# The transform of the tail: per sequence, by products of 64 rows and 64 columns, on the upper and the lower half of TensorE

## The chip, the cores and the metric

The kernel runs on one core of one Trainium2 chip. A core has TensorE (PE; its weight loads are shown as PEld), VectorE (DVE), ScalarE (ACT), GpSimd (POOL) and a queue that issues DMAs (SP). The metric is the device time of one execution in microseconds: the kernel before takes 1292.83 us, the median of 3 runs that lie between 1289.83 and 1294.05.

## The reference

Two layers are computed over 128 sequences of 64 tokens with 128 channels, `x` and a context `ctx` of the same shape:

```
x = x + L0_xattn(layernorm(x), ctx, ctx)      # softmax attention, 16 heads of 8
x = x + L0_ffn(layernorm(x))                  # 64 experts, the 8 best of each token, and a shared one
x = x + L1_xattn(layernorm(x), ctx, ctx)      # the part that the change touches
x = x + L1_ffn(layernorm(x))                  # ternary weights, one product
```

The third line correlates queries and keys along the sequence by Fourier transforms, and mixes shifted copies of the values:

```
Q, K, V = _linear(query, Wq, bq), _linear(key, Wk, bk), _linear(value, Wv, bv)   # split into heads
corr = irfft(rfft(Q, axis=seq) * conj(rfft(K, axis=seq)), n=64, axis=seq)
top_w, top_idx = top_k(corr.mean(axis=-1), 4)                                    # int(log(65)) = 4 delays
out = sum_i softmax(top_w)[i] * roll(V, top_idx[i], axis=seq)
out = _linear(out, Wo, bo)
```

## The kernel before, in words

A tile is 128 rows by 128 channels: two sequences of 64 tokens, one in partitions 0 to 63, the other in 64 to 127. There are 64 tiles. Everything stays in SBUF from one layer to the next. `attention` works through the tiles first, `experts` through 33 pairs of experts in 16 chunks of tiles, then `tail` does the third layer and what precedes the fourth, and `ternary` the last product and the stores.

`tail` works on pairs of tiles, 32 pairs, in a software pipeline of 46 steps that is written out in program order for each engine. In step s the pair n = s - 1 is transformed, n = s - 2 is projected, n = s - 3 is multiplied on POOL, and so on up to the pair s - 13. What precedes what within a step is the order of the `if on(s, lag)` blocks in each engine's function; semaphores tie the engines together.

TensorE's order in a full step is: output projection of pair s - 11 (L1547, L1548), in every fourth step the transpose of the delays' weights (L1553), the transform of pair s - 1 (L1561), the inverse transform of pair s - 10 (L1573), two transposes (L1581), in every fourth step L1587, the projections of pair s - 2 (L1594 to L1596, once for each tile of the pair), and in every fourth step the correlation (L1606).

The transform is what changes. For each of the four sources of a pair (tile 0 and 1 of the normed x, tile 0 and 1 of the context) the source is the stationary operand, 128 rows of tokens by 128 channels, and a 128x128 table `cst["dft"][:, 0:P]` moves through. The table holds the two sequences' transforms in blocks, so its result has the channels as partitions and 128 columns in which frequency and sequence alternate: column 2f + b is frequency f of sequence b. Half of the table's numbers are zeros, since each sequence is transformed by itself. A product of two f32 operands is carried out as two instructions for TensorE, each with its own weight load, so the four products of a pair appear as eight loads and eight matmuls. The results of a pair fill one PSUM bank, and there are two such banks, `pf[0]` and `pf[1]`, used in turn: the transform of pair n waits until ScalarE has copied pair n - 2 out (`at_least(pe, f_out, n - 1)`). ScalarE's copy (L1501) takes the 512 columns to `l_xf` in SBUF, from which the projections read.

ScalarE's order in a step is: L1496 in every fourth step, the copy L1501, the exponential L1505 in every fourth step, L1510, L1514 in every fourth, L1520, L1526, and then the copies of the projections, L1535 to L1537 (for the first eight pairs once per tile, then once per pair).

The tables come in by DMAs that SP issues once, with the fourth tile of `attention` (L225).

Of the kernel before, what the change touches and what calls it, by code (L numbers as in the profile page):

```python
# [22 lines left out]
F32 = mybir.dt.float32  # L23
# [66 lines left out]
def attention(nc, cst, dram, x, ctxT, x_res, raw, held, norms, routing, sem, n_tiles=TILES):  # L90
# [7 lines left out]
    with ExitStack() as mem:  # L98
# [99 lines left out]
        late_weights = [(w1[:, k, :], dram[name]) for k, name in enumerate(("Wq1", "Wk1", "Wv1", "Wo1"))] + [  # L198
            (wt_raw, dram["wt"]), (bo1row[:], dram["bo1"].unsqueeze(0)), (bv1col[:], dram["bv1"].unsqueeze(1))]
        tables = [(cst["eb"][:], dram["eb"].unsqueeze(0).to_broadcast([P, E]))]  # L200
        tables += [(cst[name][:], dram[name]) for name in ("dft", "idft_corr", "idft_conv")]
        tables += [(cst[name][:], dram[name].unsqueeze(1)) for name in ("ln_gamma", "ln_beta")]
        tables += [(braw[:, k, :], dram[name].unsqueeze(0).to_broadcast([3, D])) for k, name in ((0, "bq1"), (1, "bk1"))]

# [973 lines left out]
def dft_tables():  # L1178

    f = np.concatenate([np.arange(S // 2 + 1), np.arange(1, S // 2)])
    second = np.arange(S) > S // 2
    angle = 2 * np.pi * np.outer(f, np.arange(S)) / S
    cos, sin = np.cos(angle), np.sin(angle)
    weight = np.where((f == 0) | (f == S // 2), 1.0, 2.0)[:, None] / S
    sign = np.where(second, -1.0, 1.0)[:, None]
    alone = ((f == 0) | (f == S // 2))[:, None]
    rows = lambda m: np.kron(np.eye(2), m).reshape(2, S, P).transpose(1, 0, 2).reshape(P, P)  # L1190
    cols = lambda m: rows(m).T
    return {

        "dft": np.concatenate([cols(np.where(second[:, None], -sin, cos)), cols(np.where(second[:, None], cos, -sin))], 1),

        "idft_corr": np.concatenate([rows(np.where(alone, 0.0, weight * sign * sin)), rows(weight * cos)], 1) / HD,

        "idft_conv": np.concatenate([rows(weight * sign * cos), rows(-weight * sin)], 1),
    }
# [25 lines left out]
def tail(nc, cst, entry, x_res, y_mean, y_rstd, xnT, amax, sem):  # L1225
# [15 lines left out]
    with ExitStack() as mem:  # L1241
# [3 lines left out]
        def psum(name, shape):  # L1245
            return mem.enter_context(nc.psum_tensor(name, shape, F32))
# [23 lines left out]
        y_mv = sb("l_y_mv", [P, 4, 2])  # L1270
        y_ve = sb("l_y_ve", [P, 4])

        pf = [psum(f"l_pf{i}", [P, 2, 2, P]) for i in range(2)]
        pq = psum("l_pq", [P, 2, 512])[:, :, 0:3 * D].rearrange("p j (c d) -> p j c d", d=D)
        po = psum("l_po", [P, 2, P])
        py = psum("l_py", [P, 2, D])
# [56 lines left out]
        with nc.Block() as block:  # L1333
# [155 lines left out]
            @block.scalar  # L1489
            def _(act):  # L1490
                for s in range(STEPS):
                    g = group(s, 9)
                    if g is not None:
                        act.wait_ge(w_turned, g + 1)
                        at_least(act, c_transformed, g)
                        nc.scalar.copy(cT[:], pw).then_inc(w_out, 1)  # L1496
                    if on(s, 1):
                        n = s - 1
                        act.wait_ge(transformed, n + 1)
                        at_least(act, projected, 2 * (n - 1))  # L1500
                        nc.scalar.copy(xf[:, n % 2], pf[n % 2][:]).then_inc(f_out, 1)  # L1501
                    k = group(s, 8)
                    if k is not None:
                        act.wait_ge(shifted, k + 1)
                        nc.scalar.activation(e[:], e[:], ACT.Exp).then_inc(exped, 1)  # L1505
                    if on(s, 10):
                        n = s - 10
                        act.wait_ge(inverted, n + 1)
                        at_least(act, o_projected, n - 1)
                        nc.scalar.copy(oT[:, n % 2], po[:]).then_inc(o_out, 1)  # L1510
                    if g is not None:
                        act.wait_ge(c_transformed, g + 1)
                        at_least(act, mixed, 4 * (g - 1))
                        nc.scalar.copy(cf[:, g % 2].rearrange("p i t h -> p i (t h)"), pab).then_inc(c_out, 1)  # L1514
                    if on(s, 12):
                        n = s - 12
                        act.wait_ge(rooted, 2 * n + 2)
                        at_least(act, z_turned, n - 1)
                        for j in range(2):
                            ins = nc.scalar.activation(zn[:, n % 2, j, :], x_res[:, 2 * n + j, :], ACT.Identity,  # L1520
                                                       bias=offset[:, n % 2, j:j + 1], scale=rstd[:, n % 2, j:j + 1])
                        ins.then_inc(z_normed, 1)
                    if on(s, 13) and s - 13 >= DRAINED:
                        n = s - 13
                        act.wait_ge(z_turned, n + 1)
                        nc.scalar.activation(xnT[:, 2 * n * P:2 * (n + 1) * P], pt[:], ACT.Identity,  # L1526
                                             bias=cst["ln_beta"][:], scale=cst["ln_gamma"][:]).then_inc(z_out, 1)
                    if on(s, 2):
                        n = s - 2
                        at_least(act, mixed, n - SLOTS + 1)  # L1530
                        at_least(act, products, n - SLOTS + 1)
                        for tiles in ((0, 1), (1, 2)) if n < APART else ((0, 2),):
                            some = slice(*tiles)
                            act.wait_ge(projected, 2 * n + tiles[1])
                            nc.scalar.copy(qkv[:, n % SLOTS, some, 1:4, :], pq[:, some])  # L1535
                            nc.scalar.copy(qkv[S:, n % SLOTS, some, 0, :], pq[0:S, some, 1, :])
                            nc.scalar.copy(qkv[0:S, n % SLOTS, some, 0, :], pq[S:, some, 1, :]).then_inc(q_out, tiles[1] - tiles[0])  # L1537

            @block.tensor
            def _(pe):  # L1540
                for s in range(STEPS):
# [12 lines left out]
                    if on(s, 1):  # L1554
                        n = s - 1
                        pe.wait_ge(normed, n + 1)
                        pe.wait_ge(loaded[n % 4], 16 * (n // 4 + 1))
                        at_least(pe, f_out, n - 1)
                        for j in range(2):
                            for i, src in enumerate((xn[:, n % 2, j], cin[:, n % 4, j])):  # L1560
                                ins = nc.tensor.matmul(pf[n % 2][:, j, i, :], src, cst["dft"][:, 0:P], start=True, stop=True)  # L1561
                        ins.then_inc(transformed, 1)
                    if s == 1:
                        for j in range(4):
# [146 lines left out]
def two_layers(nc, d, out):  # L1711

    with ExitStack() as mem:
        def sb(name, shape, dt=F32):
            return mem.enter_context(nc.sbuf_tensor(name, shape, dt))

        def sem(name):
            return mem.enter_context(nc.semaphore(name))

        shapes = {  # L1720
            "ident": ([P, P], F32), "hmask": ([P, 4], F32), "maskq": ([P, P], BF16),
            "maskk": ([P, 4 * S], BF16), "ones": ([P, P], F32), "mhalf": ([P, 1], F32),
            "Wq": ([D, D], F32), "Wo": ([D, D], F32), "bqc": ([P, 1], F32), "boe": ([P, D], F32),
            "centT": ([D, E], F32), "eb": ([P, E], F32),
            "w1T": ([D, 4, D], F32), "bias3": ([P, 4, D], BF16), "first_rows": ([P, P], BF16), "ones3": ([P, P], BF16),
            "dft": ([P, 2 * P], F32), "idft_corr": ([P, 2 * P], F32), "idft_conv": ([P, 2 * P], F32),
            "ln_gamma": ([D, 1], F32), "ln_beta": ([D, 1], F32), "beta": ([P, 1], F32), "wt": ([D, D], F32),
        }
        cst = {name: sb(name, shape, dt) for name, (shape, dt) in shapes.items()}
        x_res = sb("x_res", [P, TILES, D])  # L1730
        rows = "(t p) s d -> t (p s) d"
        x = d["x"].rearrange(rows, p=2)
        ctx = d["ctx"].rearrange(rows, p=2)
        y_mean = sb("y_mean", [P, TILES])
        y_rstd = sb("y_rstd", [P, TILES])
        held = sb("held", [P, 2048])
        entry = Entry(nc, held, ctx, sem)
        with ExitStack() as ffn:
            for name in ("wuh", "wul", "wdh", "wdl"):
                cst[name] = ffn.enter_context(nc.sbuf_tensor(name, [P, PAIRS * P], F32R))  # L1740
            raw = ffn.enter_context(nc.sbuf_tensor("raw", [P, 2, PAIRS * P], F32))
            norms = ChunkNorm(nc, ffn, sem)
            routing = Routing(nc, ffn, sem, cst, raw, norms)
            attention(nc, cst, d, x, d["ctxT"], x_res, raw, held, norms, routing, sem)
            experts(nc, cst, x_res, norms, routing, entry, y_mean, y_rstd, sem)
        xnT2 = sb("xnT2", [P, TILES * P])
        amax = sb("amax", [P, TILES // 2])
        tail(nc, cst, entry, x_res, y_mean, y_rstd, xnT2, amax, sem)
        ternary(nc, cst, x_res, xnT2, amax, out.rearrange(rows, p=2), sem)

# [32 lines left out]
```

## Time and profile before

| | us |
|---|---|
| median of 3 runs | 1292.83 |
| the profiled execution, its own time | 1293.18 |
| its span, first to last instruction | 1291.3 |
| first transform of the tail (L1561) | starts at 1106.7 |
| last one | starts at 1228.8 |

All times in the profile are of one execution. They count from the span's start. TensorE's granted clock, as a share of full speed, is 0.985 over the span and 1.00 from 1106 to 1230 us. A matmul's recorded duration has a fixed part in it, since matmuls overlap in the array: eight matmuls of 275 ns each take 1.06 us together, not 2.2. The pace at which they follow each other is read from the starts, or from the time of a group.

### The profile page before, as it was taken

What the parts mean: (1) busy time and instruction counts of PE and PEld (TensorE: products, weight loads), DVE (VectorE), ACT (ScalarE), POOL (GpSimd) and SP (SyncE); (2) the same over time, 40 slices, a digit from 0 to 9 for tenths busy, and PEclk for the clock granted to TensorE, in tenths of its full rate; (3) what the DMA queues carried; (4) which work ended last, traced back from release to release, by engine and by line L of the source; (5) the groups of instructions that cost most, each with busy time, mean ns of one, the idle gap of its engine ahead of it and who ended that gap; (6) DMA issues with size and microseconds to landing.
All of it is one profiled execution on the core that took longest, in us unless ns stands there. A gap on an engine that the chain in (4) does not pass through costs nothing. (4 is left out here: it accounts for less than half of the span.)

```text
span 1291.3 us, 29811 instructions
## 1 busy us (share of the span) xinstructions
PE 1240.9 (96%) x9114; PEld 998.2 (77%) x9114; DVE 1066.5 (83%) x2061; ACT 922.4 (71%) x1525; POOL 769.2 (60%) x828
## 2 busy tenths in 40 slices
PE   7999999996999999999999999999999999899986
PEld 4777777775788888788878878788878888799975
DVE  4878888886788879779879889779889787689986
ACT  3778888884777777676767777777777777777761
POOL 3775665662556556656657556656657533477773
PEclk9999999997999999999999999999999999999998
DMA  4511111100976776876866876876877777111004
GB/s 119 114 31 31 30 28 32 29 20 3 213 184 165 184 181 154 193 169 151 195 162 171 192 170 165 189 175 160 186 169 178 184 181 182 34 34 30 22 2 131
DMA packets 126149, 159.56 MB, mean 124 GB/s; under 512 B 20840, under 2 KB 59504, under 8 KB 126064
## 3 DMA queue, kind: packets, MB, share of 16 engines
q1 hardware_dynamic: 124974, 158.16, 50.3%
q8 instruction: 34, 0.56, 0.2%
q10 hardware_dynamic: 1090, 0.43, 0.1%
q14 instruction: 51, 0.42, 0.1%
HBM read 152.25 MB, written 6.29 MB: 123 GB/s over the span
## 5 line engine op out<-in xcount | busy, mean ns | idle before, releaser
L1036 DVE TENSOR_TENSOR e_m<-e_pu,raw 128x1024 f32<-128x1024 f32 x256 | 309.8, 1211 | 94.6 <-ACT e_pu L1099 67.7
L1099 ACT ACTIVATE e_pu<-e_pu 128x1024 f32<-128x1024 f32 x256 | 258.6, 1010 | 161.7 <-PE e_pu L1135 160.0
L1109 ACT CAST e_mh<-e_m 128x1024 fp32r<-128x1024 f32 x256 | 268.0, 1047 | 46.3 <-DVE e_m L1036 45.4
L955 POOL TENSOR_TENSOR e_ml<-e_m,e_mh 128x1024 fp32r<-128x1024 f32 x80 | 192.9, 2415 | 125.3 <-ACT e_mh L1109 125.1
L1041 DVE TENSOR_TENSOR e_ml<-e_m,e_mh 128x1024 fp32r<-128x1024 f32 x176 | 238.6, 1356 | 21.6 <-ACT e_mh L1109 20.8
L1133 PE MATMUL e_pu<-r_xh,wuh 128*128 128x512 f32 x528 | 215.1, 407 | 2.3 <-PEq L208 1.9
L1144 PE MATMUL e_py<-e_mh,wdh 128*128 128x512 f32 x528 | 208.4, 395 | 3.0 <-ACT held L1086 3.0
L1134 PE MATMUL e_pu<-r_xh,wul 128*128 128x512 f32 x528 | 209.4, 397 | 0.0
L1135 PE MATMUL e_pu<-r_xl,wuh 128*128 128x512 f32 x528 | 209.3, 396 | 0.0
L1145 PE MATMUL e_py<-e_mh,wdl 128*128 128x512 f32 x528 | 209.1, 396 | 0.0
L1148 PE MATMUL e_py<-e_ml,wdh 128*128 128x512 f32 x528 | 168.2, 397 | 1.0 <-DVE e_ml L1041 0.4
L1144 PEld LDWEIGHTS e_py<-e_mh,wdh 128*128 128x128 f32 x528 | 99.1, 188 | 27.7 <-issue 4.2
L1148 PEld LDWEIGHTS e_py<-e_ml,wdh 128*128 128x128 f32 x528 | 98.1, 188 | 28.6 <-POOL e_ml L955 4.1
L1133 PEld LDWEIGHTS e_pu<-r_xh,wuh 128*128 128x128 f32 x528 | 99.8, 189 | 25.1 <-issue 2.3
L1135 PEld LDWEIGHTS e_pu<-r_xl,wuh 128*128 128x128 f32 x528 | 99.8, 189 | 24.2
L1145 PEld LDWEIGHTS e_py<-e_mh,wdl 128*128 128x128 f32 x528 | 99.1, 188 | 24.4
L1134 PEld LDWEIGHTS e_pu<-r_xh,wul 128*128 128x128 f32 x528 | 100.0, 189 | 21.1
L377 POOL TENSOR_TENSOR kx<-qkT,hmask 128x512 f32<-128x512 f32 x64 | 66.5, 1039 | 80.2 <-ACT qkT L479 78.3
L267 DVE TENSOR_REDUCE mx<-ps 128x16 f32<-128x1024 f32 x64 | 78.3, 1224 | 43.3 <-PE ps L530 43.3
L569 PEld LDWEIGHTS pob<-vx,pT 128*64 128x64 f32 x2048 | 66.2, 139 | 27.7 <-issue 21.2
L272 DVE TENSOR_TENSOR prob<-ps,mx 128x1024 f32<-128x1024 f32 x64 | 77.6, 1212 | 0.1
L569 PE MATMUL pob<-vx,pT 128*64 128x18 f32 x2048 | 72.4, 214 | 2.3 <-DVE x_res L289 1.5
(232 smaller groups left out, 2358.5 us busy)
## 6 DMA issues: line engine op xcount, KB each, us to landing
raw<-gates_scratch SPq DMA_DIRECT2D x512, 256.0 KB, 4.3
x_res<-in_x_dram SPq DMA_DIRECT2D x64, 64.0 KB, 1.8
xcT<-in_ctxT_dram SPq DMA_DIRECT2D x64, 64.0 KB, 1.9
held<-in_ctx_dram SPq DMA_DIRECT2D x32, 128.0 KB, 2.1
out_dram<-t_res SPq DMA_DIRECT2D x16, 256.0 KB, 2.8
raw<-in_L_ffn_W_up_dram SPq DMA_DIRECT2D x4, 512.0 KB, 4.3
raw<-in_L_ffn_W_down_dram SPq DMA_DIRECT2D x4, 512.0 KB, 5.8
gates_scratch<-raw SPq DMA_DIRECT2D x16, 128.0 KB, 2.3
```

Source lines behind the costliest of these rows:

```text
L569: ins = nc.tensor.matmul(po[q, 2 * j:2 * j + 2, :], pT[:, r % 2, j, q], vx[:, r % 4, j, b], start=True, stop=True)
L955: nc.gpsimd.tensor_tensor(flat(ml[k][:]), flat(m[k][:]), flat(mh[k][:]).bitcast(F32), ALU.subtract).then_inc(m_low[1], 1)
L1036: nc.vector.tensor_tensor(flat(m[r % 3][:]), flat(pu[r % 3][:]), flat(gt[i % SPREAD]), ALU.mult).then_inc(gated, 1)
L1041: nc.vector.tensor_tensor(flat(ml[k][:]), flat(m[k][:]), flat(mh[k][:]).bitcast(F32), ALU.subtract).then_inc(m_low[0], 1)
L1099: nc.scalar.activation(flat(pu[k][:]), flat(pu[k][:]), ACT.Silu).then_inc(silued, 1)
L1109: nc.scalar.copy(flat(mh[k][:]), flat(m[k][:])).then_inc(m_high, 1)
L1133: nc.tensor.matmul(pu[k][:, j, :], cst["wuh"][:, w], xh[:, b, :], start=True, stop=False)
L1134: nc.tensor.matmul(pu[k][:, j, :], cst["wul"][:, w], xh[:, b, :], start=False, stop=False)
L1135: ins = nc.tensor.matmul(pu[k][:, j, :], cst["wuh"][:, w], xl[:, b, :], start=False, stop=True)
L1144: nc.tensor.matmul(py[:], cst["wdh"][:, w], mh[k][:, j, :], start=(i == 0 and j == 0), stop=False)
L1145: nc.tensor.matmul(py[:], cst["wdl"][:, w], mh[k][:, j, :], start=False, stop=False)
L1148: ins = nc.tensor.matmul(py[:], cst["wdh"][:, w], ml[k][:, j, :], start=False, stop=(i == FULL))
```

## The change

The two sequences of a tile are transformed by products of their own. Each takes 64 rows of the source (partitions 0 to 63, or 64 to 127) as the stationary operand, 64 rows by 128 channels, and moves a 64x64 table through, which stands twice in `dft_half`, once in each half of the partitions. The product for sequence 0 lies on the upper half of TensorE's rows and writes to the first bank of `pf`, the one for sequence 1 on the lower half and to the second bank. There are so eight products of 64 rows and 64 columns a pair instead of four of 128 rows and 128 columns.

Both banks now belong to one pair, so there are no longer two buffers: the transform of pair n waits until pair n - 1 has been copied out. ScalarE's copy reads both banks in one instruction of 512 columns and writes them with a stride of two, so that `l_xf` looks as before. One more table, 32 KB, is loaded at the start.

```diff
-        tables += [(cst[name][:], dram[name]) for name in ("dft", "idft_corr", "idft_conv")]
+        tables += [(cst[name][:], dram[name]) for name in ("dft", "dft_half", "idft_corr", "idft_conv")]
...
+        "dft_half": np.tile(np.where(second[:, None], -sin, cos).T, (2, 1)),
...
-        pf = [psum(f"l_pf{i}", [P, 2, 2, P]) for i in range(2)]
+        pf = psum("l_pf", [P, 2, 512])[:, :, 0:4 * S].rearrange("p b (a f) -> p b a f", f=S)
...
-                        nc.scalar.copy(xf[:, n % 2], pf[n % 2][:]).then_inc(f_out, 1)
+                        nc.scalar.copy(xf[:, n % 2].rearrange("p j i (f b) -> p b (j i) f", b=2), pf).then_inc(f_out, 1)
...
-                        at_least(pe, f_out, n - 1)
+                        at_least(pe, f_out, n)
                         for j in range(2):
                             for i, src in enumerate((xn[:, n % 2, j], cin[:, n % 4, j])):
-                                ins = nc.tensor.matmul(pf[n % 2][:, j, i, :], src, cst["dft"][:, 0:P], start=True, stop=True)
+                                for b in range(2):
+                                    rows = slice(S * b, S * b + S)
+                                    ins = nc.tensor.matmul(pf[:, b, 2 * j + i, :], src[rows], cst["dft_half"][rows], start=True, stop=True)
```

On TensorE, at the tail's start, before the change (`l_pf` is the transform's PSUM, `held` the sources, `l_pd` and `l_pq` PSUM of other stages):

```order
L1561 MATMUL l_pf<-dft,held 128x128 [waits n_loaded0,n_normed]
L1561 MATMUL l_pf<-dft,held 128x128 x3
L1565 MATMUL l_pd<-ident,held 128x128 x4
L1561 MATMUL l_pf<-dft,held 128x128 [waits n_loaded1,n_normed]
L1561 MATMUL l_pf<-dft,held 128x128 x3
L1594 MATMUL l_pq<-w1T,l_xf 128x128 [waits l_f_out]
```

The same place after it; lines from L1200 on stand two lower, from the transform's own loop on four:

```order
L1565 MATMUL l_pf<-dft_half,held 128x64 [waits n_loaded0,n_normed]
L1565 MATMUL l_pf<-dft_half,held 128x64 x7
L1569 MATMUL l_pd<-ident,held 128x128 x4
L1565 MATMUL l_pf<-dft_half,held 128x64 [waits l_f_out,n_loaded1,n_normed]
L1565 MATMUL l_pf<-dft_half,held 128x64 x7
L1598 MATMUL l_pq<-w1T,l_xf 128x128 [waits l_f_out]
```

Four products became eight of half the columns, and the second pair's transform waits for `l_f_out`, the first pair's copy, as it did not before.

A full step of the tail on TensorE before, from the output projection to the first inverse transform:

```order
L1547 MATMUL l_py<-w1T,l_oT 128x128 [waits l_added,l_o_out]
L1547 MATMUL l_py<-w1T,l_oT 128x128
L1548 MATMUL l_py<-bias,ones 128x256
L1561 MATMUL l_pf<-dft,held 128x128 [waits l_f_out,n_loaded2,n_normed]
L1561 MATMUL l_pf<-dft,held 128x128 x3
L1573 MATMUL l_po<-idft_conv,l_rr 128x128 [waits l_o_out,l_mixed]
```

And after:

```order
L1549 MATMUL l_py<-w1T,l_oT 128x128 [waits l_added,l_o_out]
L1549 MATMUL l_py<-w1T,l_oT 128x128
L1550 MATMUL l_py<-bias,ones 128x256
L1565 MATMUL l_pf<-dft_half,held 128x64 [waits l_f_out,n_loaded2,n_normed]
L1565 MATMUL l_pf<-dft_half,held 128x64 x7
L1577 MATMUL l_po<-idft_conv,l_rr 128x128 [waits l_o_out,l_mixed]
```

Nothing else moves: the half-height products stand between products over all 128 rows, in every one of the 32 steps that transform a pair.

## Rows read from the trace of the kernel before

**Rows 1.** The page: the span, TensorE's busy time, share and instructions.

```profile
span 1291.3 us, 29811 instructions
PE 1240.9 (96%) x9114; PEld 998.2 (77%) x9114; DVE 1066.5 (83%) x2061; ACT 922.4 (71%) x1525; POOL 769.2 (60%) x828
```

**Rows 2.** Busy time of each engine in two stretches of the tail.

```profile
core 0: us, PE busy (x) PEld busy (x) DVE busy (x) ACT busy (x) POOL busy (x), PEclk, DMA share, GB/s
1166.00:1184.00 18.00, 17.85 (x146) 16.38 (x145) 17.38 (x62) 14.14 (x32) 13.76 (x22) 1.00 0.11 31
1184.00:1202.00 18.00, 17.85 (x146) 16.39 (x145) 17.38 (x61) 14.14 (x32) 13.77 (x21) 1.00 0.11 31
```

**Rows 3.** Waits from 1129 to 1231 us: total, times, longest.

```profile
ACT l_qkv L1535 <- PE l_pq L1596: 11.3, 17, 1.2
...
PEld l_pd L1553 <- DVE l_w L1411: 1.7, 4, 0.4
```

**Rows 4.** The matmuls of L1561: ns min/median/max, first and last start.

```profile
L1561 PE MATMUL l_pf<-dft,held x256: 275/275/348, 1106.8 to 1228.9; 128*128 128x128 f32 x128
```

**Rows 5.** Timeline of a full step: start, us, engine, line, tiles, count.

```profile
1174.76 0.97 PEld L1561 LDWEIGHTS l_pf<-dft,held 128*128 128x128 f32 x8
...
1174.76 0.27 PE L1548 MATMUL l_py<-bias,ones 128*128 128x256 bf16 x1
1174.87 1.06 PE L1561 MATMUL l_pf<-dft,held 128*128 128x128 f32 x8
1175.76 0.50 PE L1573 MATMUL l_po<-idft_conv,l_rr 128*128 128x128 f32 x3
```

**Rows 6.** Full-height loads with 64 moving columns: L746, timeline and durations.

```profile
328.42 0.86 PEld L746 LDWEIGHTS e_pt<-centT,raw 128*128 128x128 f32 x7
...
L746 PE MATMUL e_pt<-centT,raw x120: 217/275/275, 328.4 to 1013.4; 128*128 128x64 f32 x120
```

**Rows 7.** Timeline of one attention tile, where half and quarter heights follow each other.

```profile
201.67 0.39 PE L574 MATMUL pob<-Wo,oT 128*128 128x128 f32 x2
201.99 0.40 PE L526 MATMUL ps<-maskk,maskq 64*128 64x256 bf16 x4
202.31 0.69 PE L530 MATMUL ps<-kx,qkT 32*64 32x256 f32 x16
...
201.98 0.12 PEld L526 LDWEIGHTS ps<-maskk,maskq 64*128 64x128 bf16 x4
202.31 0.23 PEld L530 LDWEIGHTS ps<-kx,qkT 32*64 32x64 f32 x16 [0.21 <-issue]
```

**Rows 8.** Lines by shape: busy, mean ns of one.

```profile
L569 PEld LDWEIGHTS pob<-vx,pT 128*64 128x64 f32 x2048 | 66.2, 139 | 27.7 <-issue 21.2 <-DVE x_res L289 5.2 <-ACT pT L464 1.4
...
L530 PEld LDWEIGHTS ps<-kx,qkT 32*64 32x64 f32 x1024 | 15.2, 133 | 14.1 <-issue 14.1
```

**Rows 9.** The matmuls of L530 in that tile: min/median/max.

```profile
L530 PE MATMUL ps<-kx,qkT x16: 374/400/425, 202.3 to 202.6; 32*64 32x256 f32 x16
```

**Rows 10.** Timeline of the tail's first steps.

```profile
1107.94 0.58 ACT L1501 COPY l_xf<-l_pf 128x512 f32<-128x512 f32 x1 [1.62 <-PE l_pf L1561]
...
1108.07 0.97 PEld L1561 LDWEIGHTS l_pf<-dft,held 128*128 128x128 f32 x8
...
1110.61 1.06 PE L1561 MATMUL l_pf<-dft,held 128*128 128x128 f32 x8
...
1113.03 1.06 PE L1561 MATMUL l_pf<-dft,held 128*128 128x128 f32 x8
...
1120.76 1.06 PE L1561 MATMUL l_pf<-dft,held 128*128 128x128 f32 x8
...
1123.79 1.06 PE L1561 MATMUL l_pf<-dft,held 128*128 128x128 f32 x8
...
1125.02 0.59 ACT L1501 COPY l_xf<-l_pf 128x512 f32<-128x512 f32 x1
...
1128.53 0.33 PE L1553 MATMUL l_pd<-ident,l_w 128*128 128x128 f32 x1 [2.15 <-DVE l_w L1411]
```

**Rows 11.** Timeline, ACT and PEld: a copy of 768 columns, a fourth step's stall.

```profile
1174.14 0.80 ACT L1535 COPY l_qkv<-l_pq 128x768 f32<-128x768 f32 x1 [0.68 <-POOL l_rr L1329]
...
1175.96 0.58 ACT L1501 COPY l_xf<-l_pf 128x512 f32<-128x512 f32 x1 [0.27 <-PE l_pf L1561]
...
1179.27 0.14 PEld L1553 LDWEIGHTS l_pd<-ident,l_w 128*128 128x128 f32 x1 [0.43 <-DVE l_w L1411]
```

More of the change, by code:

```diff
@@ L1725, in two_layers @@
             "w1T": ([D, 4, D], F32), "bias3": ([P, 4, D], BF16), "first_rows": ([P, P], BF16), "ones3": ([P, P], BF16),
-            "dft": ([P, 2 * P], F32), "idft_corr": ([P, 2 * P], F32), "idft_conv": ([P, 2 * P], F32),
+            "dft": ([P, 2 * P], F32), "dft_half": ([P, S], F32), "idft_corr": ([P, 2 * P], F32), "idft_conv": ([P, 2 * P], F32),
             "ln_gamma": ([D, 1], F32), "ln_beta": ([D, 1], F32), "beta": ([P, 1], F32), "wt": ([D, D], F32),
```

## The prediction

> **What bounds the kernel now.** I read the page first: TensorE is busy for 96% of the span [rows 1], so any time of its own counts unless it waits where the change lies. The change touches only the tail, where L1561 runs from 1106.8 to 1228.9 us [rows 4]. So the second view is the busy time by stretch: from 1166 to 1202 us TensorE is busy 17.85 of each 18 us, VectorE 17.38, ScalarE 14.14, POOL 13.8, at a clock of 1.00 [rows 2]. Since recorded matmuls overlap, that alone does not prove a full engine; the third view does. In the waits, ScalarE waits for TensorE (11.3 us), while TensorE's one stall of weight is L1553, which waits for VectorE's delay weights, 4 times, 1.7 us in all [rows 3]. The timeline shows everything else back to back [rows 5]. So in the 23 steps between the ninth and the last transform TensorE sets the pace, with VectorE 3.5% behind it: each nanosecond added to a transform lengthens a step, and one saved is worth something only down to VectorE's 17.38/18.
>
> **The transform, before.** In rows 5 L1548 starts at 1174.76, the eight matmuls of L1561 at 1174.87, L1573 at 1175.76. So L1548's 256 bf16 columns hold the array for 0.11 us, and a transform takes 0.89, or 8 slots of 0.112. From L1548's start to L1573's it is 1.00 us.
>
> **What a slot costs with 64 columns.** The change hopes for slots of half the length. L746 is the row to ask: full-height f32 loads of 128 columns, each with a matmul of only 64 moving columns. Seven loads there take 0.86 us, and one takes 0.19, so they follow each other by (0.86 - 0.19)/6 = 0.112 us [rows 6]: the same as with 128 moving columns. Its matmuls need less (217 ns at the least, 275 for L1561's: 0.058 less for 64 columns fewer [rows 4, 6]), and still the slot does not shrink: the load of 128 columns sets it. Before, load and matmul are of equal length and hide each other; after, the loads are twice as many and each has its 128 channels as columns as before. Does a load get cheaper with half the rows? L569's, 128 rows by 64 columns, take 139 ns, L530's, 32 rows by 64, 133 [rows 8]: no.
>
> **Do the two halves run beside each other?** In L530, on quarter heights, 16 loads of some 0.13 us each take 0.23 together, and 16 matmuls of 256 f32 columns take 0.69 [rows 7], where one after the other would need 16 x 0.22. So parts of the array load and multiply in parallel. With two halves, 16 loads are 8 slots of 0.112 = 0.89 us: what it was. The best that the products can do is to cost the same.
>
> **The changes of height.** Each transform now stands between full-height products, so the array is regrouped 64 times. The attention tile shows what that costs [rows 7]. L574's second matmul starts at 201.67 + 0.39 - 0.275 = 201.79, streams 0.11, and L526's load comes only at 201.98: 0.08. L526's last starts at 202.12, streams 0.11, and L530's load comes at 202.31, "issue" before it: 0.08, unrounded about 0.09. In the steady step a load starts while the matmul before it streams; here it starts 0.09 after its end, and is no longer hidden either: the first matmuls of L530 take 425 ns, the later 374 [rows 9], 0.05 for a load of 64 columns, so 0.11 for one of 128. Bounds for one change of height: 0.08 (gap alone, load hidden elsewhere) and 0.23 (gap 0.12, load 0.11). I take 0.20, the two rows' values added.
>
> **Sum of a step.** L1548 streams 0.11, gap 0.09, eight load slots 0.89, the last 64-column matmul 0.06, gap 0.09, exposed load of L1573 0.11: 1.35 us from L1548 to L1573, against 1.00. Plus 0.35 a step.
>
> **The new wait.** The transform of pair n now waits for the copy of pair n - 1 (`f_out`). In a full step that copy runs from 1175.96 to 1176.54 [rows 11] and the next transform is at 1179.3: nothing. At the start it bites once: the copy of pair 0 ends at 1107.94 + 0.58 = 1108.52, and the second transform, which began at 1108.07 [rows 10], would begin at some 1108.6. Behind it on TensorE stand the first projections, and behind these ScalarE's copies: 0.5 us.
>
> **The first steps.** From the third to the fourth transform it is 2.42 us, TensorE's own time; from there to the seventh (1113.03 to 1120.76) 2.58 a step, which is ScalarE's: 0.16 of slack [rows 10]. So the shift grows by 0.5, then 0.35 twice, then 4 x (0.35 - 0.16) = 0.76: about 2.0 at the copy of 1125.02, which ends the long wait of 2.15 us before L1553 (copy, exponential, VectorE's chain). The projections in between vanish in that wait, the shift of 2.0 does not.
>
> **The steady steps.** 23 intervals and the last transform itself, 24 x 0.35 = 8.4. Off that go the four stalls of L1553, 0.43 the longest [rows 3, 11]: VectorE's chain to it starts from the correlation a step earlier, so a slower TensorE meets it later, 4 x 0.35 = 1.4 absorbed. What stays is 7.0. Some 0.3 more I let go in the drain after 1229, where VectorE has no backlog to work off.
>
> **ScalarE's copy** reads two banks at once (L1535's 768-column copy does, 0.80 us against 0.58 for 512: 0.83 ns a column [rows 11]) and writes with a stride of two, which no row shows. Bounds: 0, and a second 0.83 ns for each of 512 columns, 0.43. I take 0, since it is one element after the other either way. With 0.43, ScalarE has 14.14 + 1.7 of 18 and still isn't the bound; the first steps would lose 0.23 x 5 and the chain 0.4, +1.6 in all. **The extra table** is one issue on SP in the first microseconds of attention, and its buffer 256 bytes a partition: 0, with at most its one issue of half a microsecond if SP's cover there were gone.
>
> 2.0 + 7.0 - 0.3 = +8.7 us. The profiled execution took 1293.18, so 1301.9; that execution lies 0.35 above the median, so against the median I say 1301.5.
>
> **Rivals.**
> (A) The halves load one after the other: 16 slots of 0.112, 0.89 more for each of 32 transforms, less the first one: +28 on top, 1330. Against it stand the 16 loads in 0.23 us of rows 7, though those have 64 columns and smaller heights. 7%.
> (B) In split rows a load does not hide behind a matmul of its own half: slot 0.112 + 0.056, +0.45 for some 28 transforms, 1314. In rows 5 eight loads and eight matmuls of the same rows fit in 1.1 us, so full height hides them; that split height does is argued from L530's 16 loads, all out before the first matmuls end [rows 7]. 7%. The Trainium skill (TensorE: Matmul & The Clock Gate, Part 3, The mechanism) says that a weight load overlaps running matmuls only where the row group differs; rows 5 contradict it for this kernel, and B is what it would give.
> (C) The slot does shrink to 0.056, but the changes of height stay: 1.35 - 0.45 = 0.90 against 1.00, -0.1 a step, +0.5 for the start: -1.5, 1291.3, no change that can be told. Against it: rows 6. 8%.
> (D) The other side: slots of 0.056 and the regrouping hidden. A transform would save 0.45, but VectorE is the bound from 17.38/18 on, 0.15 of a 4.44 us step, x 23 = 3.5, and ScalarE's 2.58 holds the first steps; with the drain some 4.4: 1288.5. It decides in its favour if a half-height load is shorter than 0.08. 5%. The Trainium skill (TensorEngine Tiling, Theoretical Speedup) promises up to twice the throughput where the contraction is 64 or less. By that rule alone the products would take 0.45 us; rows 6 say that this kernel's slot is not made of moving columns.
> The forecast has the rest, 73%.
>
> **How the numbers follow.** With 0.08 for a change of height the step costs 0.11 and the whole some 3.5; with 0.23, 0.41 and +10.5; with the slow copy +12. So the forecast's own range is 1296.5 to 1305. To leave out no more than 2 in 10 I go down to 1294, short of C and D, and up to 1312, to the edge of B. What a measurement of this kernel can tell from no change is 0.3%, 3.9 us. Faster: D and a little of C, 0.06. Same: C, and the forecast's lower end, 0.10. Slower: 0.84.
>
> **What would show it.** Right: loads of the transform 0.11 apart in each half, in pairs; a transform with its neighbours 1.35 from L1550 to L1577; gaps of 0.09 with nothing to wait for before its first load and before L1577's; L1553's stall gone or under 0.1; the last transform about 9 us later, the rest of the tail unchanged. Wrong: pairs 0.056 apart (C, D), 0.17 (B), or 16 loads one by one (A); no gap at the changes of height; or a copy of over 0.7 us.

## The result, and the profile after

| | kernel before | changed kernel |
|---|---|---|
| median, 7 executions each | 1292.83 us | 1304.70 us |
| range | 1289.83 to 1294.31 | 1299.90 to 1309.14 |
| profiled execution | 1293.18 | 1299.90 |
| its span | 1291.3 | 1298.1 |

The ratio is 1.0087, 95% interval 1.0073 to 1.0101: slower by 11.2 us by the ratio, where 8.7 were forecast. With two later sets (five and three executions) the changed kernel has 15 executions, their median is 1301.1 us.

The page after, answering to [rows 1]:

```profile
span 1298.1 us, 30324 instructions
PE 1248.4 (96%) x9370; PEld 1000.9 (77%) x9370; DVE 1072.1 (83%) x2061; ACT 924.2 (71%) x1525; POOL 768.6 (59%) x828
```

256 more matmuls and as many loads, and 7.5 us more of TensorE. The busy time of the same two stretches, answering to [rows 2]:

```profile
core 0: us, PE busy (x) PEld busy (x) DVE busy (x) ACT busy (x) POOL busy (x), PEclk, DMA share, GB/s
1166.00:1184.00 18.00, 18.00 (x169) 15.77 (x168) 16.92 (x61) 13.49 (x31) 12.60 (x21) 1.00 0.11 31
1184.00:1202.00 18.00, 18.00 (x169) 15.84 (x168) 16.92 (x59) 13.27 (x29) 13.06 (x20) 1.00 0.11 31
```

TensorE shows no idle time any more (the recorded matmuls overlap and cover the gaps that the loads show below), every other engine has more, and the loads are busy for less of the time. A full step, first TensorE's matmuls, then its loads (start, us, engine, line, tiles, count), answering to [rows 5]:

```profile
1177.85 0.27 PE L1550 MATMUL l_py<-bias,ones 128*128 128x256 bf16 x1
1178.05 1.11 PE L1565 MATMUL l_pf<-dft_half,held 64*128 64x64 f32 x16
1179.09 1.16 PE L1577 MATMUL l_po<-idft_conv,l_rr 128*128 128x128 f32 x8
```

```profile
1177.73 0.10 PEld L1550 LDWEIGHTS l_py<-bias,ones 128*128 128x128 bf16 x1
1178.05 0.97 PEld L1565 LDWEIGHTS l_pf<-dft_half,held 64*128 64x128 f32 x16 [0.21 <-DVE held L1222]
1179.09 0.97 PEld L1577 LDWEIGHTS l_po<-idft_conv,l_rr 128*128 128x128 f32 x8
1179.97 0.14 PEld L1585 LDWEIGHTS l_pt<-ident,l_zn 128*128 128x128 f32 x1
```

Sixteen loads take 0.97 us, as eight did: they run in pairs, 0.112 apart. L1550 starts at 1177.85 and streams for 0.11; the first half-height load comes at 1178.05, a gap of 0.09. At the other end L1577's eight matmuls take 1.16 instead of 1.06, since their first load is not hidden. That load starts 0.20 us after the last half-height matmul does (its recorded start is 1178.885); these 64 columns stream for 0.06 (from the last L1564 matmul to the next load, full height, below), so the gap here is 0.14. The releaser named beside the gap, VectorE's L1222, is not the cause: elsewhere the same 0.21 is put down to "issue", as in the waits from 1126 to 1228 us (total, times, longest):

```profile
PEld l_pf L1565 <- issue: 3.5, 17, 0.3
...
PEld l_pd L1555 <- DVE l_w L1413: 2.3, 1, 2.3
```

Only the first and long stall of L1555 is left; the four later ones of [rows 3] are gone. The copy, answering to [rows 10, 11] (ns min/median/max, first and last start), is somewhat longer, 0.636 us in the median instead of 0.585:

```profile
L1503 ACT COPY l_xf<-l_pf x32: 621/636/647, 1104.3 to 1235.4; 128x512 f32<-128x512 f32 x32
```

The distance from one transform to the next, from the starts of the first loads, in us. The executions without and with a fall of the clock are two profiled executions of the same changed kernel:

| transforms | before | changed, no fall | changed, first profile |
|---|---|---|---|
| 1 to 2 | 1.33 | 1.91 | 1.91 |
| 2 to 3, 3 to 4 | 2.43, 2.43 | 2.80, 2.77 | 2.80, 2.77 |
| 4 to 7, each | 2.57 | 2.77 | 2.77 |
| 8 to 9 | 4.92 | 4.96 | 4.96 |
| 9 to 10 | 2.90 | 3.21 | 4.82 |
| four steady steps | 4.54, 4.09, 4.54, 4.58 | 4.88, 4.43, 4.88, 4.54 | 4.88, 4.43, 4.88, 4.54 |
| 1 to 32, in all | 121.28 | 129.52 | 131.12 |

(Transform 32 of the kernel before starts at 1228.03; the 1228.8 of the table before is its last load.) Three of four steady steps are 0.34 longer, the fourth is 0.04 shorter. From the first to the last transform the profiled execution lost 9.84 us, but its whole span is only 6.8 longer, because its first transform came 3.6 us earlier (1103.1, not 1106.7). Then there is something that the prediction did not have: behind the stall of L1555 one step takes 4.82 us. The granted clock (column PEclk) shows why, in three stretches of the first profile after:

```profile
1104.00:1127.60 23.60, 21.52 (x207) 17.25 (x204) 16.87 (x43) 20.59 (x53) 9.10 (x10) 1.00 0.16 45
1127.60:1131.00 3.40, 3.40 (x21) 2.92 (x20) 3.02 (x6) 1.18 (x3) 2.01 (x3) 0.51 0.15 43
1131.00:1240.00 109.00, 108.99 (x1004) 95.75 (x1002) 95.86 (x332) 80.59 (x180) 76.20 (x115) 1.00 0.09 25
```

For 3.4 us TensorE ran at its lower level, 1.2 instead of 2.4 GHz, at a cost of 1.61 us. The kernel before had 1.00 from 1106 to 1240.

### The profile page after: what moved, and what is told of

It is laid out like the page before. It is cut to its first block and busy times, and to the rows that moved or that the text cites. A ratio compares the mean times of both kernels' runs of the same rounds, so it can differ in the third digit from the quotient of the medians.

```text
span 1298.1 us, 30324 instructions
## 1 busy us (share of the span) xinstructions
PE 1248.4 (96%) x9370; PEld 1000.9 (77%) x9370; DVE 1072.1 (83%) x2061; ACT 924.2 (71%) x1525; POOL 768.6 (59%) x828
```

## The experiments

The kernels of one set ran on one chip and shared the executions of the kernel before.

**The changed kernel once more** (no edit).

> The changed kernel once more, beside the others. Theory (eight load slots of 0.112 us as before, two changes of height at 0.17 to 0.2 each, one wait at the start): 1.34 to 1.35 us from L1550 to L1577 in every full step, the tail 8.5 to 11 us longer than before. The tail of the profiled execution was 10.6 us longer, 1.9 of them in the one step after the long stall of L1555, where TensorE's granted clock fell to half for 3.4 us. Rival for that part: chance, the clock drop does not come again and the ratio is nearer 1.007 than 1.009.

Ratio 1.0078 (1.0064 to 1.0092), median 1300.53 against 1291.74. The profiled execution has a clock of 1.00 throughout the tail's steps, and is the middle column of the table above. From L1550's start to the load after the inverse transform it is again 2.13 us, 0.34 more than before (1.79). From L1550's start to L1577's first load it is 1.24, and that load, no longer hidden, adds 0.11: the 1.35 expected. So the fall of the clock is no fixed part of the change.

**The wait alone.** In the kernel before:

```diff
-                        at_least(pe, f_out, n - 1)
+                        at_least(pe, f_out, n)
```

> The kernel before with only the wait of the change: the transform of pair n waits for the copy of pair n - 1. Theory: 0.5 us once, at the second transform, some of it won back in the following steps, since ScalarE sets their pace: 0 to +0.6 us. Rival (the loss of the second buffer is what costs): +8 us.

Ratio 1.0009 (1.0000 to 1.0018). In the trace, the second transform comes 0.57 us later, and 0.56 of it is still there at the last transform: nothing else waits, and nothing is won back either. I had expected part of it back from ScalarE's pace; but ScalarE's work is behind the same wait and, as I read it, moves with it: every later distance is as before. The clock did not fall in its steps.

**Full height, 64 columns.**

```diff
-                                    rows = slice(S * b, S * b + S)
-                                    ins = nc.tensor.matmul(pf[:, b, 2 * j + i, :], src[rows], cst["dft_half"][rows], start=True, stop=True)
+                                    ins = nc.tensor.matmul(pf[:, b, 2 * j + i, :], src, cst["dft_half"][:, S * b:S * b + S],
+                                                           start=True, stop=True)
```

> The eight products of 64 moving columns into two banks, but each with all 128 rows as stationary operand (table with the two sequences' columns apart), so no change of height and no halves beside each other. Result as the reference's. Theory (a slot is the load of 128 columns, 0.112 us, whatever moves): 16 slots, 1.79 us a transform instead of 0.89, no gap before or after: +24 to +28 us. Rival (a slot is made of moving columns, 0.056): a transform of 0.9, +0.5 to +1 us.

Ratio 1.0220 (1.0204 to 1.0236), +28 us. The step's loads and matmuls:

```profile
1182.05 1.86 PEld L1564 LDWEIGHTS l_pf<-dft_half,held 128*128 128x128 f32 x16
1183.83 0.97 PEld L1577 LDWEIGHTS l_po<-idft_conv,l_rr 128*128 128x128 f32 x8
```

```profile
1182.04 0.27 PE L1550 MATMUL l_py<-bias,ones 128*128 128x256 bf16 x1
1182.15 1.90 PE L1564 MATMUL l_pf<-dft_half,held 128*128 128x64 f32 x16
1183.89 1.11 PE L1577 MATMUL l_po<-idft_conv,l_rr 128*128 128x128 f32 x8
```

The same sixteen pairs of load and matmul with 64 moving columns take 1.86 us when they use all rows, 0.97 in halves. That is the whole worth of the halves beside each other, and it only makes good the doubled number of loads. There is no gap: L1564's first matmul starts 0.11 after L1550's, and L1577's first load 0.06 after L1564's last matmul.

**Twice the moving columns.** In the changed kernel:

```diff
-        "dft_half": np.tile(np.where(second[:, None], -sin, cos).T, (2, 1)),
+        "dft_half": np.tile(np.where(second[:, None], -sin, cos).T, (2, 2)),
...
-        pf = psum("l_pf", [P, 2, 512])[:, :, 0:4 * S].rearrange("p b (a f) -> p b a f", f=S)
+        pf = psum("l_pf", [P, 2, 4, P])
```

with the copy reading `pf[:, :, :, 0:S]`.

> The changed kernel with a table of 64x128 instead of 64x64: each of the eight half-height products moves 128 columns, the second 64 of which are not used (output unchanged). Theory (the load sets the slot): slots stay 0.112, only the last matmul is 0.056 longer: +0.056 x 28 = +1.6 us on the changed kernel. Rival (moving columns set it): slots twice as long, +0.45 x 28 = +12 on it.

Ratio 1.0086 (1.0071 to 1.0102), beside 1.0078 of the changed kernel on the same chip. The times alone can't tell 1.6 us; the trace does:

```profile
1180.68 0.97 PEld L1565 LDWEIGHTS l_pf<-dft_half,held 64*128 64x128 f32 x16 [0.21 <-issue]
1181.77 0.97 PEld L1577 LDWEIGHTS l_po<-idft_conv,l_rr 128*128 128x128 f32 x8
```

The loads still take 0.97. Each steady step is 4.49, 4.93 or 4.60 us instead of 4.43, 4.88 or 4.54: 0.05 to 0.06, the last matmul. So an island of half-height products costs 0.39 us against the kernel before (4.93 against 4.54) when its last matmul is not a short one. Its clock fell too, at 1130.2.

**Half the loads.** In the changed kernel, the context's products are left out; each load of a normed source serves 128 columns (the table's second copy is not shown):

```diff
-                            for i, src in enumerate((xn[:, n % 2, j], cin[:, n % 4, j])):
-                                for b in range(2):
-                                    rows = slice(S * b, S * b + S)
-                                    ins = nc.tensor.matmul(pf[:, b, 2 * j + i, :], src[rows], cst["dft_half"][rows], start=True, stop=True)
+                            src = xn[:, n % 2, j]
+                            for b in range(2):
+                                rows = slice(S * b, S * b + S)
+                                ins = nc.tensor.matmul(pf[:, b, 2 * j:2 * j + 2, :], src[rows], cst["dft_half"][rows], start=True, stop=True)
```

> The changed kernel with four half-height products a pair instead of eight, each with one load and 128 moving columns (the context's transforms are left out, the table stands twice). As many moving columns as in the changed kernel, half the loads, as many changes of height. Theory (a slot is set by its load): 4 slots instead of 8 in each half, 0.39 to 0.45 us less a transform than the changed kernel: 0.95 us from L1550 to L1577, and -1 to +1.5 us against the kernel before. Rival (moving columns set it): as the changed kernel, +10 us.

Ratio 1.0002 (0.9991 to 1.0014). With as many moving columns as the changed kernel, half the loads take

```profile
1182.99 0.52 PEld L1565 LDWEIGHTS l_pf<-dft_half,held 64*128 64x128 f32 x8 [0.21 <-issue]
1183.63 0.97 PEld L1577 LDWEIGHTS l_po<-idft_conv,l_rr 128*128 128x128 f32 x8
```

and the loss is gone, to the 0.05 us a step that the sum expects (steps of 4.49 and 4.04 us, 4.54 and 4.09 before). So even with half of the transforms left out, this form only draws level: the changes of height eat what is saved. This is as near as a kernel comes to rival C's case, half the slot time with the changes of height kept: it would have meant no change.

**More changes of height.** In the changed kernel, half the inverse transform goes between the products of the two tiles, in 23 steps, and is left out at its old place (not shown):

```diff
                         for j in range(2):
+                            if j == 1 and on(s, 10):
+                                pe.wait_ge(mixed, s - 9)
+                                at_least(pe, o_out, s - 10)
+                                for i in range(2):
+                                    nc.tensor.matmul(po[:, 0, :], rr[:, (s - 10) % 2, i, 0, :], cst["idft_conv"][:, i * P:i * P + P],
+                                                     start=(i == 0), stop=(i == 1))
```

> The changed kernel with half of the inverse transforms (full height, L1566 here) moved between the products of tile 0 and those of tile 1 of the transform: in 23 steps two more changes of height, and no more work. Result as the reference's. Theory (a pair of changes costs 0.34 us on a full TensorE): 23 x 0.34 = +7.8 us on the changed kernel, some 1.0135 to 1.015 of the kernel before. Rival (the 0.34 is the cost of split products as such, or of the copy and the wait, not of changing): 0 to +1 us on it.

Ratio 1.0134 (1.0117 to 1.0151), just under the range expected. The step:

```profile
1180.85 0.27 PE L1550 MATMUL l_py<-bias,ones 128*128 128x256 bf16 x1
1181.06 0.66 PE L1571 MATMUL l_pf<-dft_half,held 64*128 64x64 f32 x8
1181.65 0.71 PE L1566 MATMUL l_po<-idft_conv,l_rr 128*128 128x128 f32 x4
1182.29 0.66 PE L1571 MATMUL l_pf<-dft_half,held 64*128 64x64 f32 x8
1182.88 0.71 PE L1583 MATMUL l_po<-idft_conv,l_rr 128*128 128x128 f32 x4
```

Steps are 4.77, 5.22 and 4.88 us instead of 4.43, 4.88 and 4.54: another 0.34 for two more changes and no other work. The last transform comes 15.72 us later than before, relative to the first; without the added changes 8.24. The difference of 7.5 is 22 x 0.34, as only 22 of the 23 steps lie ahead of the last transform. That is the price of regrouping, apart from the split products, the copy and the wait.

**What a shorter transform would be worth.** In the kernel before, the context's transforms are left out (the copy that takes the normed ones for them is not shown):

```diff
-                            for i, src in enumerate((xn[:, n % 2, j], cin[:, n % 4, j])):
-                                ins = nc.tensor.matmul(pf[n % 2][:, j, i, :], src, cst["dft"][:, 0:P], start=True, stop=True)
+                            ins = nc.tensor.matmul(pf[n % 2][:, j, 0, :], xn[:, n % 2, j], cst["dft"][:, 0:P], start=True, stop=True)
```

> The kernel before, with only the two normed sources of a pair transformed, the copy takes them for the context's too: four loads and matmuls a pair instead of eight, 0.45 us less of TensorE in each of 32 transforms, no change of height (the context's transforms are left out). It asks what a shorter transform would have been worth. Theory (VectorE is 3.5% behind TensorE, ScalarE sets the first steps): 3.5 to 5 us faster, VectorE busy over 99% of a stretch in the middle. Rival (TensorE alone bounds the tail): 0.45 x 28 = 12.5 us faster.

Ratio 0.9959 (0.9944 to 0.9975), 5.3 us faster, a little over the range expected. TensorE's 0.45 a transform would be 14 us in all; nearly two thirds are lost. VectorE was expected to be busy for over 99%; its busy time in a stretch is what it was, 17.35 of 18:

```profile
1160.00:1178.00 18.00, 17.22 (x137) 15.48 (x137) 17.35 (x63) 14.75 (x34) 14.10 (x21) 1.00 0.11 31
1178.00:1196.00 18.00, 17.20 (x138) 15.47 (x137) 17.38 (x65) 14.22 (x34) 14.18 (x21) 1.00 0.13 38
```

Two steps of four are 0.45 shorter, the other two hardly: in the one the correlation waits for VectorE's sums, in the other L1553 for its weights, twice as long as before [rows 11]. The last three lines are VectorE's own, around that wait:

```profile
1171.15 0.52 PEld L1605 LDWEIGHTS l_pd<-idft_corr,l_sums 128*128 128x128 f32 x4 [0.54 <-DVE l_sums L1464]
...
1176.70 0.14 PEld L1553 LDWEIGHTS l_pd<-ident,l_w 128*128 128x128 f32 x1 [0.92 <-DVE l_w L1411]
...
1176.15 0.17 DVE L1407 RECIPROCAL l_wrec<-l_wsum 128x2 f32<-128x2 f32 x1
1176.36 0.29 DVE L1411 TENSOR_TENSOR l_w<-l_w,l_wrec 128x128 f32<-128x128 f32 x1
1176.56 0.68 DVE L1464 TENSOR_REDUCE l_sums<-l_pp 128x64 f32<-128x512 f32 x1
```

VectorE waits for nobody here. From the 13th to the 29th transform (67.51 us) it pauses 71 times between instructions, never for more than 0.035 us, and these pauses, 2.44 us, are its whole idle time, 3.6%. TensorE's two waits in each group of four steps are both for VectorE's results. So it is VectorE that sets the pace, at a busy share of 96.4%; the share was a wrong sign for it. In the kernel before, the same 16 steps took 71.03 us, with 0.72 of 3.16 us idle in two longer pauses. Most of the rest of the 3.5 us came out of instructions that were recorded longer there: L1451 took 0.43 to 0.81 us, here it takes 0.44 to 0.54. Why is not known.

**Looking for the slower executions.** Three more profiled executions of the changed kernel, no edit.

> The changed kernel, one profiled execution, to catch one above 1303 us. Of 12 executions 5 lay there, at mean granted clocks of 0.98, none of the kernel before. Theory (the half-height products and the gaps around them lower TensorE's activity, so its clock falls for 3.4 us at a time within the tail's steps, some 1.6 us each): a slow execution shows two to five such drops between 1104 and 1240 us, a fast one none or one. Rival (the drops lie in attention or between the stages, which the change does not touch): drops before 1100 us, the tail as long as in the fast ones.

> As look1, a second execution of the changed kernel: above 1303 us with two to five clock drops inside the tail's steps by the theory, with the drops before 1100 us by the rival; a fast one tells neither.

> As look1, a third execution of the changed kernel: above 1303 us with two to five clock drops inside the tail's steps by the theory, with the drops before 1100 us by the rival; a fast one tells neither.

They took 1303.54, 1303.69 and 1300.72 us. All three have two falls of the clock in the tail, and the same ones. Stretches of the first:

```profile
1106.00:1109.50 3.50, 2.64 (x36) 2.39 (x36) 0.60 (x2) 0.81 (x2) 0.00 (x0) 1.00 0.13 37
1109.50:1112.90 3.40, 3.40 (x14) 2.25 (x11) 1.20 (x3) 1.62 (x4) 0.00 (x0) 0.50 0.14 39
1112.90:1133.40 20.50, 18.63 (x179) 15.08 (x179) 15.66 (x38) 18.55 (x49) 9.84 (x10) 1.00 0.14 40
1133.40:1136.80 3.40, 3.40 (x13) 2.80 (x14) 2.32 (x5) 1.83 (x5) 1.88 (x3) 0.50 0.15 43
```

Before the first fall TensorE waits at the tail's start and then for the copy, before the second it waits at L1555. Here is what precedes the first one (timeline of TensorE):

```profile
1106.64 1.11 PE L1565 MATMUL l_pf<-dft_half,held 64*128 64x64 f32 x16 [1.08 <-PEq L923]
1107.68 0.66 PE L1569 MATMUL l_pd<-ident,held 128*128 128x128 f32 x4
1108.56 1.18 PE L1565 MATMUL l_pf<-dft_half,held 64*128 64x64 f32 x16 [0.23 <-ACT l_xf L1503]
```

The first fall makes its step 4.42 us instead of 2.80, the second 4.86 instead of 3.21: from the first to the last transform it is 132.8 us, where the execution without a fall has 129.5 and the kernel before 121.3. The expectation that tied falls to executions over 1303 us did not hold: the third execution has both and took 1300.72, while its tail began 4 us earlier (first transform at 1102.4 us, not 1106.6 and 1106.9). Over the fourteen profiled executions of all these kernels, that start lies between 1102.4 and 1107.7. Both falls lie in the tail, where the theory had them, but only behind idle stretches (2.7 to 2.9 us after TensorE went on at the tail's start, 0.8 to 1.5 after it went on at L1555), never in a steady step. Two falls cost 3.3 us. The executions of 1304.7 to 1309.1 us, five of the first twelve, stay without an explanation: none of them was profiled.

**Products in the idle time.** First at L1555 alone, then also before the first two transforms, with full-height products whose results nobody reads. The second version:

```diff
+                        if n < 2:
+                            for _ in range((6, 2)[n]):
+                                nc.tensor.matmul(py[:, 0, :], cst["dft"][:, 0:P], cst["dft"][:, 0:P], start=True, stop=True)
                         pe.wait_ge(normed, n + 1)
...
+                        if g == 0:
+                            for _ in range(7):
+                                nc.tensor.matmul(py[:, 0, :], cst["dft"][:, 0:P], cst["dft"][:, 0:P], start=True, stop=True)
                         pe.wait_ge(weights, g + 1)
```

> The changed kernel, with seven full-height products (1.57 us, results not used) before L1555's first wait, the only long one inside the steps (1.87 us idle). Theory (the clock fell in that stall in the profiled execution, 1.6 us lost in the step behind it, because TensorE idled and had regrouped before): the clock stays at 1.00 through the steps; the ninth step is 3.2 us as in the execution without the drop, and the mean comes 0 to 1.6 us below the changed kernel's, by the share of its executions that drop. Rival (the drop has nothing to do with the stall): it comes here too in some executions, no difference in the ratio. Rival 2: the fillers themselves delay what follows, +0.3 us or more.

> The changed kernel with full-height products (results not used) in all three idle stretches of TensorE where its clock was seen to fall behind: seven before L1555's first wait, six before the first transform, two before the second. Three of three further executions of the changed kernel had both drops in the tail, near 1109 and 1132 us, 3.5 us of time in all; one of the first two had only the second, one none. Theory (idle time at the tail's start and at L1555 makes the clock fall, the half-height steps alone don't): no drop before 1240 us, the last transform 8.2 to 8.6 us later than before, relative to the first, and a ratio of 1.0055 to 1.0065, against 1.0078 and 1.0087 without fillers. Rival (the drops come from the half-height products): the drops stay in some executions, the ratio stays at 1.0075 or more.

With the fill at L1555 the ratio is 1.0061 (1.0041 to 1.0081), and one of six executions still took 1305.84. With all three it is 1.0076 (1.0063 to 1.0089), six executions between 1299.62 and 1301.54. In both profiled ones the clock stays up throughout, as in this stretch of the second:

```profile
1104.00:1240.00 136.00, 134.76 (x1247) 117.09 (x1246) 114.88 (x375) 100.60 (x231) 86.49 (x124) 1.00 0.10 29
```

and the last transform comes 8.38 us late (8.24 with the first), where the falls cost 1.6 each. At the tail's start the fill missed its aim, though:

```profile
1106.14 1.41 PEld L1563 LDWEIGHTS l_py<-dft 128*128 128x128 f32 x12 [1.31 <-issue]
1107.67 0.64 PEld L1571 LDWEIGHTS l_pf<-dft_half,held 64*128 64x128 f32 x10
```

TensorE still idles for 1.3 us, and then the added products run for 1.4: the first transform starts 2.83 us after the last expert product, in all the other thirteen profiled executions 1.44. The fill makes the kernel 1.39 us slower there, 0.0011 of its time if it is passed on in full. That may be why the ratio is 1.0076, the rival's figure, and not 1.0065 at most. Its interval covers both ratios without a fill: a gain in time is not shown. Nor is it shown that the fill keeps the clock up. Neither of the two filled executions has a fall up to its last transform, but of the eight executions with half-height products and no fill three have none either (one of the changed kernel, those with half the loads and with more changes), and the first filled one has none at the tail's start, where it has no fill.

## Why the prediction was right

**The bound.** TensorE set the pace, and a transform's extra time went into the step one to one. That VectorE limits a faster TensorE was right too, and that it would do so soon; "3.5% behind" was a wrong reading of it. These 3.5% were nearly all pauses of up to 0.035 us between instructions, and they stayed when VectorE set the pace. The steps got 5.0% shorter (71.03 to 67.51 us in 16), not 3.5, since some of its instructions were recorded shorter then.

**The slot.** The load sets it. Full height with 64 columns (16 loads in 1.86 us), half height with 128 (0.97), and half the loads (0.52) agree with 0.112 a load whatever moves. That L746 already showed it, among full-height products, was enough to rule out the hoped-for halving [rows 6].

**The halves** do run beside each other, loads too: sixteen loads in 0.97. Rival A is out. Rival B is out as well: with 0.168 a slot the loads would take 1.4, and with 128 moving columns in each half, where it would need 0.22 a slot, they still take 0.97. The rule of the Trainium skill behind B (TensorE: Matmul & The Clock Gate, Part 3, The mechanism) is not what the trace shows here; a load hides behind a matmul of its own half.

**The changes of height.** 0.35 a step was forecast, 0.34 measured, and 0.34 once more in the experiment that adds two changes. From the start of the last matmul to the first load of the other height it is 0.20 us at every change, after 64 f32 columns (0.06 of streaming) as after 128 or after 256 bf16 ones (0.11), so the gap was 0.09 at the one end and 0.14 at the other; the exposed load was 0.10 to 0.11. The sum comes out all the same, since the last matmul starts 0.06 before its slot is over, where the forecast put it behind the slot. The Trainium skill says that changing the tiling mode drains TensorE (TensorEngine Tiling, Key Properties) without a price; here it is 0.17 us a change, the saving on the last short matmul taken off, and 0.20 with 128 moving columns, where there is no such saving.

**The wait** cost 0.57 us once, against 0.5.

**The first steps** were forecast at 2.0 up to the long stall and came to 2.10 at the ninth transform, **the stalls absorbed** 4 x 0.38 = 1.5, not 1.4. One step more, from transform 11 to 12, grew by 0.20 only. From the first to the last transform that makes 8.24 without a fall of the clock; the forecast's terms up to there (2.0 and 23 x 0.35, less 1.4) give 8.65. Its 0.3 for the drain can't be told: from the last transform's start to the end it is 63.3 us before and 62.2 to 63.9 in the five executions of the changed kernel, some of them with a fall of the clock there and some without.

**The copy** took 0.05 us more, between the bounds, and only the second transform waited for it, in the new wait.

**What was missing** is TensorE's clock. It fell behind one or both of two idle stretches, the tail's start and L1555, in 4 of 5 profiled executions of the changed kernel, 1.6 us each time. The kernel before idles at both places too (1.46 us before its first transform, 2.15 at L1553) and kept its clock there in its one profiled execution and in those with the wait alone and with half the transforms; so did the full-height kernel with 64 columns. The fall is neither in the sum nor among the rivals. Whether it makes up what lies between 8.7 and the 11.2 us of the first seven executions is not shown: the only one of them that was profiled took 1299.90 with one fall.

So the mechanism was right in its parts, and the time is right partly by luck. The medians of the two sets are 11.9 and 8.8 us above those of the kernel before, and the median of all fifteen, 1301.1, lies at the forecast 1301.5, though nothing in the sum stands for the clock, nor for the start of the tail, which moves by up to 5 us from one execution to another.

No version that beats the kernel before came out of this: every form tried with half-height products pays for two changes of height, and with the sources as stationary operands the fewest loads are the eight that it has. A form with the table stationary and the sources moving was not tried.

## What to carry to other kernels

Before a stationary operand is split by rows, ask which of load and matmul sets the slot: here a load of 128 columns took the same time at 64 rows as at 128, and splitting by rows doubles the loads. Halves beside each other win that back and no more (measured with 64 and with 128 moving columns; with a longer moving side it was not). Every island of half-height products among full-height ones costs 0.34 to 0.39 us on a full TensorE; such products belong together in few, long runs. And an engine with a busy share of 96% can be full: ask for its longest pause and for who waits for it, not for its share.

## What the runs showed of the hardware that was not expected

- TensorE's granted clock fell to half for 3.4 us, 0.8 to 2.9 us after the end of an idle stretch of 1 to 2 us, in 4 of 5 executions of the changed kernel, in 5 of 8 of all unfilled kernels with half-height products and in none of 4 without, never in a steady step. These are few executions, and what makes the difference, half-height products or the longer pauses at the start, was not told apart.
- From the last matmul of one height to the first load of the other it is 0.20 us, start to start, whether that matmul moves 64 or 128 f32 columns; at one height it is 0.06 after 64.
- VectorE at its limit shows a busy share of 96.4%, with pauses of up to 0.035 us between its instructions.
- An f32 load of 128 columns takes 0.112 us of a half's time at 64 rows as at 128, and two halves load at the same time at no loss.
- ScalarE's copy of 512 columns from two banks with a stride of two in the output takes 0.636 us, 0.585 from one bank without it.
